# Sigmoids of u ahead of those of z, and one idle step less before the scan, in a four-layer kernel

## The reference

```python
xz = hidden_states @ in_proj_w.T
x, z = jnp.split(xz, 2, axis=-1)
xc = conv(x) + conv_b                      # causal, 4 taps, one channel at a time
u = silu(xc)
dt_low, Bp, Cp = jnp.split(u @ x_proj_w.T, [DT_RANK, DT_RANK + D_STATE], axis=-1)
delta = softplus(dt_low @ dt_proj_w.T + 2 * dt_proj_b)
# state = exp(delta * A) * state + delta * B * u, for 16 states; y = sum of C * state
y = (y + u * D) * silu(z)
return y @ out_proj_w.T
```

## Time and profile before

| | |
|---|---|
| median of 3 runs | 1401.64 us (1400.54 to 1412.11) |
| the profiled execution | 1411.83 us |
| its span on the chip | 1410.0 us |
| granted TensorE clock, mean | 0.776 |
| busy: TensorE, VectorE, ScalarE | 905.6, 972.0, 594.3 us |

### The profile page before, as it was taken

The page is one execution under the profiler, slowest core; times in us unless marked ns, Lnnn a source line. Parts: engine busy times, 40 slices in busy tenths (PEclk is TensorE's granted clock), DMA queues, the critical chain, the costliest instruction groups (busy, mean ns, idle before and its releaser), DMA issues.

```text
span 1410.0 us, 29222 instructions
## 1 busy us (share of the span) xinstructions
PE 905.6 (64%) x11808; PEld 545.3 (39%) x11808; DVE 972.0 (69%) x2254; ACT 594.3 (42%) x1299; POOL 84.2 (6%) x56
## 2 busy tenths in 40 slices
PE   4655656777567577788566677777657566472554
PEld 2444535444334244445234244444334244240122
DVE  5345543655689987656699987655689987335985
ACT  3333332466633332476633332466643331445320
POOL 0000000011000000020000000011000000030630
PEclk8556858599758889697768889698658789676897
DMA  4110110311223210311223210211223310302420
GB/s 143 31 40 10 33 39 10 66 35 39 67 68 87 69 31 18 67 36 37 67 68 87 69 31 12 57 42 39 66 63 86 76 31 10 68 1 62 112 67 8
DMA packets 84822, 72.19 MB, mean 51 GB/s; under 512 B 24528, under 2 KB 63440, under 8 KB 84496
## 3 DMA queue, kind: packets, MB, share of 16 engines
q1 hardware_dynamic: 84688, 70.34, 19.7%
HBM read 66.51 MB, written 3.80 MB: 50 GB/s over the span
## 4 chain that ended last, share of the span: by engine, by line
DVE 33%; PE 20%; ACT 12%; issue 11%; DMA 3%; SPq 2%; DVEq 0%; POOL 0%; ACTq 0%; POOLq 0%
DVE SG L1727 5%; PE bank L716 3%; PE bank L543 2%; DVE Y L1820 2%; DVE XP L1740 2%; PE bank L874 2%; DVE CV L1740 2%; SPq L480 2%; ACT QBD L1063 2%; DVE bank L1727 1%; PE bank L748 1%; PE bank L824 1%; ACT relu_s L1027 1%; DVE big L1715 1%; DVE big L1702 1%
## 5 line engine op out<-in xcount | busy, mean ns | idle before, releaser
L716 PE MATMUL bank<-onehot,tparts 128*32 128x256 bf16 x3840 | 134.8, 300 | 45.3 <-DVE onehot L1506 41.6
L716 PEld LDWEIGHTS bank<-onehot,tparts 128*32 128x32 bf16 x3840 | 108.7, 105 | 80.3 <-issue 70.7
L874 PE MATMUL bank<-XP,CO 128*128 128x512 f32 x128 | 86.1, 809 | 60.6 <-DVE XP L1738 33.2
L1727 DVE TENSOR_TENSOR_SCAN SG<-big 128x512 f32<-128x512 f32 x96 | 111.7, 1205 | 0.9
L1215 ACT ACTIVATE big<-DEL,Aneg 128x512 f32<-128x512 f32 x96 | 63.8, 715 | 102.5 <-DVE SG L1727 96.7
L1027 ACT ACTIVATE relu_s<-bank,nml 128x192 f32<-128x192 f32 (+1 forms) x128 | 52.9, 426 | 112.0 <-DVE nml L1472 112.0
L874 PE MATMUL bank<-CV,CO 128*128 128x512 f32 x128 | 77.3, 735 | 32.4 <-DVE CV L1740 20.4
L1467 DVE TENSOR_REDUCE ml<-bank 128x2 f32<-128x384 f32 (+1 forms) x64 | 33.8, 569 | 71.1 <-PE bank L651 38.5
L1506 DVE TENSOR_SCALAR onehot<-ib,CO 128x1024 bf16<-128x1024 f16 x160 | 69.5, 477 | 15.7 <-PE bank L716 14.5
L748 PE MATMUL bank<-GT,QBD 128*32 128x32 f32 x3072 | 56.6, 208 | 34.9 <-DVE G L1515 22.1
L543 PE MATMUL bank<-CO,relu_s 128*128 128x128 f32 (+2 forms) x256 | 45.8, 339 | 44.7 <-ACT relu_s L1027 44.7
(11 more groups left out here) (306 smaller groups left out, 2002.7 us busy)
## 6 DMA issues: line engine op xcount, KB each, us to landing
BC<-bc_rows SPq DMA_DIRECT2D x128, 256.0 KB, 4.4
ib<-idx_rows SPq DMA_DIRECT2D x64, 256.0 KB, 4.1
big<-comb_rows SPq DMA_DIRECT2D x8, 1024.0 KB, 10.0
rows_bounce<-RO SPq DMA_DIRECT2D x256, 8.5 KB
W<-w SPq DMA_DIRECT2D x1, 2818.0 KB, 14.8
RB<-rows_bounce SPq DMA_DIRECT2D x16, 136.0 KB, 2.1
X<-x SPq DMA_DIRECT2D x4, 256.0 KB, 3.0
out<-CV SPq DMA_DIRECT2D x4, 256.0 KB, 2.3
```

The lines of the kernel that those rows point to most:

```text
L716: m = mm(bank[2 + c % 2][32 * bb:32 * bb + 32, 256 * kind:256 * kind + 256], tparts[:, kt, part, 32 * kind:32 * kind + 32], onehot[:, n % ...
L874: mm(bank[5 + j][:, :], ident, hC[(n - 1) % 2][:, j, :], start=(n == 1), stop=(n == DS)).then_inc(ysum.sem, ysum.up())
L1727: m = dve.tensor_tensor_scan(state, decay, dBu[:, n % 2, j, :], 0.0, ALU.mult, ALU.add)
```

## The change

u's sigmoids stand ahead of z's on ScalarE, and u's products ahead of z's on VectorE. The wait of TensorE ahead of the x projection is one `yield` shorter, ScalarE and VectorE have one idle step less, and SCAN_IN_PHASES is 9, which SyncE and GpSimd count by. So from here on every step of rest meets an attention step that is one earlier. The steps of TWICE keep their numbers.

```diff
--- before.py
+++ after.py
@@ -850,7 +850,7 @@
                 for k in range(2, 4):
                     pe.wait_ge(xz_sb.sem, xz_sb.at(b, k - 1))
                     mm(bank[3 + k][:, :], w("inp")[:, k * P:(k + 1) * P], XRT[:, :], start=True, stop=True).then_inc(xz_ps.sem, xz_ps.up())
-                for _ in range(3):
+                for _ in range(2):
                     yield
                 pe.wait_ge(u_ok.sem, u_ok.at(b, 2))
                 pe.sem_inc(hold_pe, 1)
@@ -1178,14 +1178,13 @@
                     act.wait_ge(xz_ps.sem, xz_ps.at(b, k + 1))
                     A(XP[:, k, DCONV - 1:], bank[5 + k][:, :], ACT.Copy).then_inc(xz_sb.sem, xz_sb.up())
                 yield
+                for j in range(2):
+                    act.wait_ge(cv_ok.sem, cv_ok.at(b, j + 1))
+                    sigmoid(CV[:, j, :], eu[:, j, :], U[:, j, :], ue_ok)
+                yield
                 for k in range(2):
                     act.wait_ge(xz_ps.sem, xz_ps.at(b, k + 3))
                     sigmoid(bank[5 + k][:, :], ez[:, k, :], SZ[:, k, :], ze_ok)
-                yield
-                for j in range(2):
-                    act.wait_ge(cv_ok.sem, cv_ok.at(b, j + 1))
-                    sigmoid(CV[:, j, :], eu[:, j, :], U[:, j, :], ue_ok)
-                yield
                 yield
                 act.wait_ge(xd_ps.sem, xd_ps.at(b, 1))
                 A(XD[:, :], bank[7][0:40, :], ACT.Copy).then_inc(xd_sb.sem, xd_sb.up())
@@ -1678,16 +1677,15 @@
                         dve.wait_ge(done.sem, done.now(b))
                 yield
                 for j in range(2):
-                    dve.wait_ge(ze_ok.sem, ze_ok.at(b, j + 1))
-                    TT(SZ[:, j, :], SZ[:, j, :], bank[5 + j][:, :], ALU.mult).then_inc(sz_ok.sem, sz_ok.up())
-                yield
-                for j in range(2):
                     dve.wait_ge(ue_ok.sem, ue_ok.at(b, j + 1))
                     TT(U[:, j, :], U[:, j, :], CV[:, j, :], ALU.mult).then_inc(u_ok.sem, u_ok.up())
                     dve.wait_ge(u_ok.sem, u_ok.now(b))
+                yield
+                for j in range(2):
+                    dve.wait_ge(ze_ok.sem, ze_ok.at(b, j + 1))
+                    TT(SZ[:, j, :], SZ[:, j, :], bank[5 + j][:, :], ALU.mult).then_inc(sz_ok.sem, sz_ok.up())
                 for _ in range(3):
                     yield
-                yield
                 dve.wait_ge(dt_sp.sem, dt_sp.at(b, 1))
 
 
@@ -1895,7 +1893,7 @@
 SET_VEC = 11
 
 KEY_PHASES, TILE_PHASES, MERGE_PHASES = 4, 14, 3
-ROUTE_PHASES, EXPERT_PHASES, NORM_PHASES, SCAN_IN_PHASES, SCAN_OUT_PHASES, TOP1_PHASES = 2, 18, 2, 10, 3, 8
+ROUTE_PHASES, EXPERT_PHASES, NORM_PHASES, SCAN_IN_PHASES, SCAN_OUT_PHASES, TOP1_PHASES = 2, 18, 2, 9, 3, 8
 TWICE = (33, 39, 56)
 TOP1_BANKS = ((5, 6), (2, 3), (5, 6), (7, 5))
```

More of the change, by code:

```diff
@@ L1180, in rest @@
                 yield
-                for k in range(2):
-                    act.wait_ge(xz_ps.sem, xz_ps.at(b, k + 3))
-                    sigmoid(bank[5 + k][:, :], ez[:, k, :], SZ[:, k, :], ze_ok)
-                yield
                 for j in range(2):
@@ L1188, in rest @@
                 yield
+                for k in range(2):
+                    act.wait_ge(xz_ps.sem, xz_ps.at(b, k + 3))
+                    sigmoid(bank[5 + k][:, :], ez[:, k, :], SZ[:, k, :], ze_ok)
                 yield
```

## The result

| | before | after |
|---|---|---|
| median, runs beside each other | 1406.88 us (4 runs) | 1433.47 us (4 runs) |
| ratio | | 1.0172, 95% 1.0130 to 1.0215 |
| the same once more | 1411.30 us (17 runs) | 1430.37 us (6 runs) |
| ratio | | 1.0147, 95% 1.0118 to 1.0175 |
| profiled execution, two for after | 1411.83 us | 1425.96 and 1426.77 us |

The change makes the kernel 1.5 to 1.7% slower, by 21 to 24 us by the ratios (19 to 27 by the medians). I had forecast 1416 (1396 to 1424): slower was the right side, but the size was too small and the time fell outside the range. Taken over the first profiled execution of each kernel alone the difference is 14.1, my sum to the tenth.

The account below looks back on a forecast made before the run. VectorE, busy 96.8 of 101 us in the woven scan, was taken as the bound, so the edit acts only through waits. Terms -3.5 + 0.7 + 9.9 + 7.0 = +14.1 on the 1401.64 median gave 1416 us, range 1396 to 1424.

Parts of the forecast that it names:

- 1. The last rest: Last rest, running alone: u's sigmoids first let the x projection start sooner, its copy held by z's sigmoids; -3.5 us.
- 2. Softplus and the scan's start: Woven rows: softplus ends earlier, but the query's rotation and a wait for scores come behind; +0.7 us in all.
- 3. The start of the picks: Tile 3's first picks wait for XRT behind QBD, 5.2 us later; balance +3.3 a row, +9.9 us for three rows.
- (d): Rival: slower still, because tile 3's picks start at 1.2 GHz; 7 us more, 1423 us; chance 0.10.
- 4. The row's end: Row's end: L897 ahead of L760 on TensorE makes L760 5.3 us later and delays the merge; +7.0 us together.
- (a): Rival: only the row's end pays, the loss at the picks' start being absorbed; 1406 us; chance 0.20.
- (b): Rival: both losses are covered and only the last rest's gain counts; 1398 us; chance 0.10.
- (e): Rival: the change doesn't do what it says, since the projection was not waiting for u; 1402 us; chance 0.03.
- (c): Rival: faster, as products and a sum fill VectorE's wait for the score matmuls at the row's end; 1387 us; chance 0.12.

Follow-up runs that it names:

- front-only run: The changed kernel with TWICE = (39, 56), without 33, so rest gives up its one-step lead there: ratio 0.9969, 4.4 us under the kernel before.

## Why the prediction was wrong, by its own steps

**1. The last rest: right.** -3.5 forecast, -3.9 and -4.0 measured, held by z's sigmoids as described.

**2. Softplus and the scan's start: wrong.** I forecast +0.7 up to the gated product and got -10.1 and -8.8. Two steps failed. The smaller: "So u ready sooner gives 0.6 us at most". XD's copy came 2.3 and 3.7 us sooner behind the norm in the second and third rows of the first profile (and 1.4 later in the first), so the polynomial started 12.3 us earlier over three rows, 11.6 in the second profile, and not 7.8. How much of that is the edit and how much the clock of one execution stays open, since the score matmuls of the third row had run at half clock in the profile of before. The larger: "What was late next ... is given up for a wait for the same scores." From the polynomial to the scan I had the rows 8.5 us longer, and they were 1.3 to 1.4 shorter: one of the two local maxima ahead of the scan, with its wait, moved behind the first scan. There it waits 1.4 to 1.7 us, and is part of the +3.6 and +4.2. The front-only run shows the gain at the scan (-14.3) and that it can't be kept when attention's steps are put back (+9.4).

**3. The start of the picks: mis-sized, and hidden by 2.** +9.9 forecast (15.6 less 5.7), +22.0 and +23.1 measured, by row 7.3 and 7.7 and not 3.3. It was the right mechanism: XRT stands behind QBD and the gap of 2.7 ahead of the second chunk is gone. In the third stretch the projection starts 0.9 us behind the gated product's end (1160.7 to 1161.6), where I let it start 0.9 ahead, which a projection of that product can't: +1.8. In the other rows and the second profile it is +1.0 to +2.2; where it is late, attention's matmuls L651 and L558 stand ahead of it. From its sum to XRT it took what I gave it within 0.3 us. The rest is the clock, 0.8 in the gate logits and some 1.5 in the first chunk of a row (2.5 in one), which I had put into rival (d) at a chance of 0.10 with 7 us. It was so in every row of every version with this start (1.67 to 1.88 us for the logits), except where TensorE was given work, which gave back 6.8 to 7.9. The Trainium skill (TensorE: Matmul & The Clock Gate, section "Why this matters for your kernels") says that idle gaps between bursts let the clock fall. The page means longer gaps than these; the trace shows the fall behind waits of 2.1 to 2.65 us too, and the run with the added matmuls bears it out; (d) deserved more than the 0.10 that I gave it. In the run with QBD behind XRT only a pause of 0.69 directly ahead was left, TensorE had been busy 1.34 of the 3.2 us before (847.0 to 850.2), and the clock was at half all the same. Terms 2 and 3 together came to +11.9 and +14.4 against my 10.6. That is luck, two errors of 10 to 13 us against each other.

**4. The row's end: what is left of the miss once 2 and 3 are set against each other.** +7.0 forecast, +12.4 and +13.5 measured. L760's delay was right in a plain row (8.0 us behind the scores' sum, forecast 2.9 + 5.3 = 8.2), 8.9 to 9.5 where the group of L897 ahead of it met the lower clock (3.0 to 3.5 us instead of 1.96); that and a slightly later sum of the scores are +1.5 to +2.3 over mine. The larger part is the step "2.1 for landing and 0.7 for the gaps": it holds in the third row (3.1 measured), but in the first two the merge stands behind L1572, which waits for the rstd: 3.0 and 5.9 us in the first profile, 4.6 and 4.5 in the second. RB's issue to `den` was 12.0 and 12.2 us over three rows, not 8.4. Of these 3.6 the earlier rstd gave back 2.3.

**The rest of the gap.** My sum of +14.1 became +20.3 and +23.8 by the distances. The ratios say 24.2 and 20.7, the medians 26.6 and 19.1. I put the sum of one execution on the median, and that was no error by itself. But outside the distances the first profile of after was 6.2 us faster than that of before: 3.4 ahead of the first row's n2 and 2.8 between `den` and the next n2; the second was 8.9 faster there, nearly all ahead of the first n2. Most of that is chance of the execution, since nothing ahead of the first n2 is touched by the edit. So the two profiled times alone would have called the forecast exact.

**The rivals.** (a), (b) and (e) are out. (c) did not happen in this kernel, but from scores to `den` 5.4 us are to be had once L760 is untied. (d) happened in all rows, and belonged in the sum.

## What to carry to other kernels

When one step of idling is taken out of interleaved work, follow the shift to the end of the row: here what it gained at its own place was real (-10 us, and -4 where nothing is woven in) and was lost more than twice over, some 110 us later, where two in-order queues met in another order. One `yield` on one engine gave most of it back, so look for the one group that stands ahead of what everybody waits for before giving up a shift. And price a new TensorE wait with the matmuls behind it at half clock, by rows of this kernel that show both; if it can't be avoided, unneeded matmuls in it may be cheaper for that stage than the idling.

## What I had not expected of the hardware

Adding 1.9 us of matmuls a row took 6.8 to 7.9 us out of the way from the gated product to the scores over three rows, with the clock at 1.00 in the first chunk instead of 0.50.

The first attention runs the same instructions in the same order before and after the change, yet it ends at quite different times, by its norm's rstd, before and then in the second profile of after:

```profile
251.49 0.21 ACT L1113 ACTIVATE rstd<-lnv 128x4 f32<-128x4 f32 x1
```

```profile
245.89 0.20 ACT L1113 ACTIVATE rstd<-lnv 128x4 f32<-128x4 f32 x1
```

The granted clock of a stretch of it differs too, again before and in the second profile of after:

```profile
60.00:120.00 60.00, 38.17 (x713) 26.00 (x707) 29.16 (x85) 22.38 (x60) 0.00 (x0) 0.59 0.10 24
```

```profile
60.00:120.00 60.00, 38.68 (x874) 26.99 (x874) 31.09 (x89) 20.30 (x57) 0.00 (x0) 0.68 0.10 24
```

That is 5.6 us ahead of anything that the edit touches. Two executions of the very same kernel do it too: in the first profile of after this rstd comes at 250.80, 4.9 us later than in the second, with a granted clock of 0.60 in that stretch. It is why effects of 2 to 4 us had to be read as distances between fixed points of one execution, and why two profiled times should not be subtracted.
